# Second attention: ACT's copies one slot earlier, query chunks in the order 3, 0, 2, 1, and the next pair's preparation shifted

## What is computed

```python
def _L1_attn_ref(hidden_states, wq_a, q_a_ln_w, wq_b, wkv_a, kv_a_ln_w, wkv_b, wo):
    NH, NOPE, ROPE_D, VH = 16, 128, 64, 128
    q = rmsnorm(hidden_states @ wq_a.T, q_a_ln_w) @ wq_b.T
    q_nope, q_pe = (q[..., :NOPE], q[..., NOPE:])          # per head
    ckv = hidden_states @ wkv_a.T
    kv = rmsnorm(ckv[..., :KV_LORA], kv_a_ln_w)            # 64 features, shared by the heads
    q_pe, k_pe = apply_rope(q_pe, cos, sin), apply_rope(k_pe, cos, sin)
    q_abs = jnp.einsum('bhsd,hdc->bhsc', q_nope, q_absorb)
    scores = (jnp.einsum('bhsc,btc->bhst', q_abs, kv)
              + jnp.einsum('bhsd,bxtd->bhst', q_pe, k_pe)) * SCALE
    scores = jnp.where(causal, scores, jnp.finfo(scores.dtype).min)
    attn = jax.nn.softmax(scores, axis=-1)
    x = jnp.einsum('bhst,btc->bhsc', attn, kv)
    x = jnp.einsum('bhsc,hdc->bhsd', x, out_absorb)
    return x.transpose(0, 2, 1, 3).reshape(b, s, NH * VH) @ wo.T
```

## Time and profile before

| | us |
|---|---|
| three runs | 1635.82, 1643.36, 1642.7 |
| median | 1642.7 |
| the profiled execution | 1639.44 |
| its span, first to last instruction | 1637.8 |
| `attend1` in it, per batch element | 337 |

### The profile page before, as it was taken

The page is one execution under the profiler, slowest core; times in us unless marked ns, Lnnn a source line. Parts: engine busy times, 40 slices in busy tenths (PEclk is TensorE's granted clock), DMA queues, the critical chain, the costliest instruction groups (busy, mean ns, idle before and its releaser), DMA issues. The chain is left out here.

```text
span 1637.8 us, 22609 instructions
## 1 busy us (share of the span) xinstructions
PE 1281.2 (78%) x7428; PEld 898.7 (55%) x7428; DVE 895.5 (55%) x2331; ACT 727.6 (44%) x1668; POOL 518.6 (32%) x556
## 2 busy tenths in 40 slices
PE   2675729889899828585899999987485999999977
PEld 2564714334344327464666666666474666666656
DVE  6645538765858243244666666650244666666640
ACT  1534404554646602443555555540334555555530
POOL 0221233332422200040555555520131554445520
PEclk8787955975959959797999999998797999999998
DMA  2313196554550086202100111005102001010005
GB/s 77 118 59 114 56 97 61 60 60 51 69 52 24 27 267 181 64 14 71 37 30 29 35 37 36 27 14 161 42 26 81 23 27 46 26 46 23 17 27 154
DMA packets 133157, 101.02 MB, mean 62 GB/s; under 512 B 48240, under 2 KB 120368, under 8 KB 132784
## 3 DMA queue, kind: packets, MB, share of 16 engines
q1 hardware_dynamic: 132000, 98.53, 26.6%
q10 hardware_dynamic: 1040, 1.05, 0.2%
HBM read 56.30 MB, written 34.87 MB: 56 GB/s over the span
## 5 line engine op out<-in xcount | busy, mean ns | idle before, releaser
L748 POOL TENSOR_SCALAR a_p<-a_p,a_rl 128x128 f32<-128x128 f32 (+7 forms) x256 | 214.9, 840 | 437.1 <-DVE a_rl L690 437.0
L731 ACT ACTIVATE a_p<-psum,a_nm 128x128 f32<-128x128 f32 (+7 forms) x256 | 189.9, 742 | 193.3 <-DVE a_nm L684 192.1
L1225 ACT ACTIVATE a_pt<-psum 128x512 f32<-128x512 f32 (+3 forms) x384 | 167.1, 492 | 148.0 <-PE psum L1098 146.2
L781 PE MATMUL psum<-ident,a_p 128*128 128x128 f32 x1152 | 186.3, 279 | 56.2 <-ACT a_pt L715 35.2
L1088 PE MATMUL psum<-a_op_k,a_op_q 64*128 64x512 f32 (+3 forms) x384 | 160.7, 511 | 51.1 <-POOL a_op_k L1023 31.7
L781 PEld LDWEIGHTS psum<-ident,a_p 128*128 128x128 f32 x1152 | 130.8, 141 | 94.1 <-ACT a_pt L715 52.5
L803 PE MATMUL psum<-a_pt,v 128*64 128x256 f32 (+1 forms) x1280 | 158.9, 370 | 2.0 <-ACT a_pt L715 2.0
L684 DVE CUSTOM_DVE_ANT_0 psum<-psum,mask_a 128x128 f32<-128x128 f32 (+3 forms) x128 | 63.8, 499 | 173.3 <-PE psum L766 173.2
L1098 PE MATMUL psum<-a_op_q,a_op_k 64*128 64x512 f32 (+3 forms) x384 | 134.8, 455 | 0.0
L1088 PEld LDWEIGHTS psum<-a_op_k,a_op_q 64*128 64x128 f32 x384 | 80.1, 236 | 87.4 <-issue 31.9
L1098 PEld LDWEIGHTS psum<-a_op_q,a_op_k 64*128 64x128 f32 x384 | 73.4, 230 | 88.9 <-ACT a_pt L1225 46.3
(11 more groups left out here) (257 smaller groups left out, 2822.6 us busy)
## 6 DMA issues: line engine op xcount, KB each, us to landing
a_swap<-a_raw SPq DMA_DIRECT2D x64, 128.0 KB, 2.3
ot_d<-a_ot SPq DMA_DIRECT2D x16, 512.0 KB, 2.6
o_ot<-ot_d SPq DMA_DIRECT2D x16, 512.0 KB, 6.3
a_raw_q<-qk_d SPq DMA_DIRECT2D x48, 128.0 KB, 5.2
a_raw_k<-qk_d SPq DMA_DIRECT2D x48, 128.0 KB, 9.2
a_wf<-wf_d SPq DMA_DIRECT2D x16, 384.0 KB, 3.3
qk_d<-p_stage_h SPq DMA_DIRECT2D x8, 512.0 KB, 2.7
qk_d<-p_stage_l SPq DMA_DIRECT2D x8, 512.0 KB, 3.4
```

The source lines that it names most:

```text
L731: e.activation(s.p[:, t % NPB, 0:(i + 1) * P], C.score[t % 2][:, 0:(i + 1) * P], ACT.Exp, scale=-1.0, bias=s.nm[:, k:k + 1], accum_out=s.l ...
L748: e.tensor_scalar(s.p[:, t % NPB, 0:(i + 1) * P], s.p[:, t % NPB, 0:(i + 1) * P], s.rl[:, k:k + 1], 1.0, ALU.mult, ALU.mult).then_inc(s.no ...
L781: ins = e.transpose(C.turn[par][:, (k - k0) * P:(k - k0 + 1) * P], s.p[:, tt % NPB, k * P:(k + 1) * P], C.ident[:, :])
L1225: e.activation(pt[:, k // G0 % NPT, hd, off:HALF], bank_b("score", g, k)[:, off:HALF], ACT.Exp, scale=-1.0).then_inc(exped, 1)
```

## The change

ACT's copies are taken from step t-4 instead of t-5; they still stand ahead of the exponential in ACT's slot, and DVE's stay at t-5. The chunks are taken in the order 3, 0, 2, 1, so the steps of a pair have 7, 8, 7, 8, then 1, 2, 1, 2, then 5, 6, 5, 6, then 3, 4, 3, 4 blocks. In a step, `c` is now the place in this order; the buffer of the transposed probabilities goes by it as before. The tables of the preparation move by two slots: PE's pieces and ACT's first four from 0, 2, 4, 6 to 2, 4, 6, 8, DVE's first two from 5, 7 to 7, 9, POOL's six from 4 to 9 to 6 to 11. ACT's pieces 4 and 5 stay in slots 12 and 13, DVE's in 13 and 14.

```diff
--- before.py
+++ after.py
@@ -598,7 +598,8 @@
 
     def __init__(self, heads, groups):
         self.heads, self.groups = heads, groups
-        self.steps = [(c, hd, 2 * c + i) for c in range(NQC) for hd in range(heads) for i in range(2)]
+        self.order = (3, 0, 2, 1)
+        self.steps = [(k, hd, 2 * c + i) for k, c in enumerate(self.order) for hd in range(heads) for i in range(2)]
         self.SG = len(self.steps)
         self.SI = 2 * self.SG
         self.per_chunk = 2 * heads
@@ -693,7 +694,7 @@
 def evacuate(e, C, s, n, t, later, parity):
 
     core = s.core
-    tt = t - LAG - 1
+    tt = t - LAG - (1 - parity)
     if (tt < 0 and not later) or tt >= core.SI:
         return
 
@@ -795,7 +796,7 @@
             e.wait_ge(s.ev_act, n * core.UG + U // 2)
             if later or cc >= len(C.out):
                 e.wait_ge(s.o_out, n * 2 * NQC + cc - len(C.out) + 1)
-        n_k = 2 * c + 2
+        n_k = 2 * core.order[c] + 2
         each = -(-n_k // core.pieces)
         for k in range(j * each, min((j + 1) * each, n_k)):
             q0 = P if k == n_k - 1 else 0
@@ -1811,10 +1812,10 @@
                 e.tensor_tensor(raw[:, t], raw[:, t], swap[:, t], ALU.add).then_inc(roped, 1)
 
 
-        AT_PE = {0: 0, 2: 1, 4: 2, 6: 3}
-        AT_ACT = {0: 0, 2: 1, 4: 2, 6: 3, 12: 4, 13: 5}
-        AT_DVE = {5: 2, 7: 3, 13: 4, 14: 5}
-        AT_POOL = {4: 0, 5: 1, 6: 2, 7: 3, 8: 4, 9: 5}
+        AT_PE = {2: 0, 4: 1, 6: 2, 8: 3}
+        AT_ACT = {2: 0, 4: 1, 6: 2, 8: 3, 12: 4, 13: 5}
+        AT_DVE = {7: 2, 9: 3, 13: 4, 14: 5}
+        AT_POOL = {6: 0, 7: 1, 8: 2, 9: 3, 10: 4, 11: 5}
 
         def next_pair(n, t, last, at):
 
@@ -1906,7 +1907,7 @@
             @block.scalar
             def _(e):
                 def place(n, g, c):
-                    return ot[:, g % 2, c * QC:(c + 1) * QC]
+                    return ot[:, g % 2, core.order[c] * QC:(core.order[c] + 1) * QC]
 
                 def slot(n, t, later, last):
                     wait_place(e, core, n, t, later, ot_out)
```

## The result

| | before | changed |
|---|---|---|
| median of four runs | 1641.2 us (1635.8 to 1643.4) | 1664.1 us (1658.6 to 1668.0) |
| ratio, 95% interval | | 1.014 [1.010, 1.018] |
| span of the profiled execution | 1637.8 us | 1666.5 us |
| second attention, per batch element | 337.2 us | 349.9 and 350.3 us |
| a middle pair of it | 42.24 us | 44.25 us |

The changed kernel is slower by 22.9 us, and the two second attentions account for 25.8 us of the 28.6 us between the profiled executions. The counts of instructions are those of the earlier trace rows: no engine was given work, though PE is busy for 15.5 us longer.

A forecast was written before the change was run, and what follows sets the result against it. PE bounds it: 37.1 of a middle pair's 42.24 us is dense work. Pairs sum to 41.1 + 6 x 44.33 + 42.6 = 349.7 against 337.3 us, +25 in both batch elements: 1664, stated as 1665, range 1652 to 1680.

The forecast's parts named there:

- First place: Slot 8: PE's transposes wait for DVE's copy of step 3, behind two remainders of the preparation; stall 1.30 us.
- Second place: Slot 14: POOL's late last rotation holds ACT's rounding, DVE's remainder and copy of step 9, then PE; stall 3.79 us.
- Slot 15: Slot 15: DVE's other remainder of the rotated rows holds its copy of step 10; PE loses 0.79 us.
- 37.05 + 0.40: Middle pair: 37.05 us dense PE work plus 0.40 us small waits in slot 13, within the pair's 44.33 us.
- The clock: PE gaps of 3.6 to 3.8 us in seven pairs per batch element bring half-clock spells, costing 1.0 us a pair.
- Rival (a): The clock does not fall, or only beside waits: 14 us less, 1651 us; chance 0.12.
- Copies ahead at no cost: ACT's copies before its exponential: the delayed exponential, nearest in slot 5, is done before scores need it, costing nothing.
- The order does help as well.: Order 3, 0, 2, 1 puts long steps beside chunk 2's weighted sums; slots 0 to 7 have no stall.
- Head and drain: Second attention's ends: first pair 40.1 + 1.0 us instead of 32.69, last pair with drain 42.6 instead of 49.87.
- (b): The clock stays low for a second spell in each pair: 18 us more, 1683 us; chance 0.10.
- (c): Last rotation ends before ACT finishes step 12; slot 14 stalls 1.4 us, pair 40.93, kernel 1617 us; chance 0.14.
- (d): Copy ahead of the exponential holds up scores, 0.5 us in each of slots 12 to 15: 1693 us; chance 0.04.

The follow-up runs named there:

- the filled kernel: Changed kernel with fourteen products of 512 columns, whose result nothing reads, added on PE in slot 14 between scores and transposes; 1651.3 us, ratio 1.007.
- first filled kernel: Changed kernel with eight products of 512 columns, whose result nothing reads, added on PE in slot 14 between scores and transposes; 1661.0 us, ratio 1.010.

## Why the prediction was right, and where not

It gave 1665 us and the kernel takes 1664.1. It put 25 us on the two attentions, and they took 25.8. Point by point:

- **First place, slot 8.** Predicted 1.30 us, measured 1.32, of DVE's copy, as said.
- **Second place, slot 14.** The last rotation was put 25.67 us behind the start of slot 4 (1367.98) and ended at 25.71 (1393.69); ACT's wait for it at 2.4, measured 2.41; the transposes at 28.77, measured 28.92 (1396.90). The gap came to 3.48 instead of 3.79, since PE was ready for it at 25.44 and not at 24.98, and the copy came 0.15 later. That this place is the cause is shown by the table of POOL alone (3.0 us a pair) and by DVE's copies ahead with the rotations still late (44.25 to 41.34), each with 1.0 of the clock in it.
- **Slot 15.** Predicted loss 0.79 us, too much. The changed kernel shows no wait of PE there, as its work at half clock fills the time; with the gap filled and no fall, 0.38 us of waiting is left. So the stalls of slots 14 and 15 came out 0.3 and 0.4 us smaller than the sum has them, while the rest of the pair without the fall is 38.1 us and not 37.05 + 0.40. That 44.33 meets 44.25 so closely is in part luck.
- **The clock.** The size was right: 1.0 us predicted, 1.01 by the filled gap; and the clock did fall in each pair. Rival (a), with 1651 us for no falls, fell with that, and the filled kernel's 1651.3 shows that it was priced rightly. The reason given was too simple. It read the gap's length as what decides. With a gap of 1.64 us the clock fell in nearly every pair of the first filled kernel, and with 1.47 in none of the kernel with POOL early, but in every second pair of one batch element with the old tables. That no gap of 1.39 to 1.68 us was followed by a fall was drawn from four cases, and the twenty longer ones leave out a gap of 9.6 us at the program's start (15.1 to 24.7), with no fall until 31.0. The trace of before could have told: the spell of 1502.15, whose price was taken, has no gap longer than 1.04 us in the 40 us ahead of it; the last above 0.5 us is the 1.01 before 1500.99, shown below the list. The Trainium skill (TensorE: Matmul & The Clock Gate, "A second HAM failure mode: psum-queue depth-cycling") tells of a kernel whose clock went up and down through short idle times between groups of products. The falls behind gaps of 1.64 and 1.01 us agree with that.
- **Copies ahead at no cost.** Nearly: with the copies alone, exponentials held up scores by 0.4 us each, 8.0 us per batch element against 4.3 before. The gain outweighs it by far, as 39.77 us a pair shows.
- **"The order does help as well."** Wrong as the effect of the order. Slots 0 to 7 of the changed kernel are nearly free of waits only thanks to the tables of PE, ACT and DVE; with the old tables and ACT's copies ahead in both, the order costs 2.4 us a pair (39.77 to 42.15). The sum did not suffer, since it was made slot by slot for the whole change.
- **Head and drain.** First pair 41.1 and 41.10, last 42.6 and 43.39; one of the falls reaches 1.2 us into the last pair, which the prediction had left at full clock.
- **Rivals.** (b) fell: one spell a pair. (c) was nearly the right price of the rotation in time: 1617 us and 40.93 a pair, against 1620.1 and 41.25 with POOL early. The 0.3 us between them fit DVE's first remainder, which took 1.58 us beside a scaling of POOL's there and 1.22 in the changed kernel. (d) didn't come.

PE in the kernel before, ahead of the spell of 1502.15, for the point on the clock:

```profile
1500.99 0.63 PE L781 MATMUL psum<-ident,a_p 128*128 128x128 f32 x4 [1.01 <-DVE a_pt L717]
```

So a middle pair lost 2.0 us: put in one after the other, the copies ahead brought 2.5, the order took 2.4, the tables of PE, ACT and DVE brought 0.9, and POOL's took 3.0, 1.0 of it by the clock. These are prices in this sequence; in another they need not be the same.

## What to carry to other kernels

Work for later that is put into an engine's program ahead of a copy that frees a buffer makes the buffer's owner wait for everything that the work waits for: put the copy first, then look for a slot for the work in which nobody waits. When a step is moved, follow the engine that does it until its last operation, since the taker may not move with it. And price a gap on PE with its clock, even one of 1.6 us. An instruction moved beside one of another engine may also take longer, as DVE's remainder did beside POOL's scaling (1.75 us against 1.22): read its duration again after the move.

## What was not expected of the hardware

The kernel with DVE's copies on the old order runs the same program for both batch elements, with the same gap of 1.52 us in slot 0 of every pair. PE in one pair of the second element:

```profile
1345.98 1.59 PE L781 MATMUL psum<-ident,a_p 128*128 128x128 f32 x7 [1.52 <-DVE a_pt L717]
```

In the first element the first six such gaps were followed by no fall (39.35 us a pair) and the seventh by one; in the second, the first by none and the last six by a fall each, at 1305.18, 1346.14 and so on, 40.96 us apart (40.91 us a pair in the stretch above). The falls in the changed kernel are 44.37 us apart (1309.37, 1353.74, 1398.12), and its pairs 44.0 to 44.7. The kernel of the new order with the old tables does the like: behind the same gap of 1.47 us in slot 14 the clock falls in every second pair of the first element and in none of the second. So whether a fall follows a gap depends on more than its length, and the same code can run on either way for six pairs. What tips it was not tried and stays open.
